# Products of constants on TensorE before each wait for gathered rows in the two relational layers

## What is computed

```python
def _rel_layer(x, src, dst, etypes, V, a, w_loop, bias, activation=None):
    W = jnp.einsum('rb,bio->rio', a, V)
    seg = dst.astype(jnp.int32) * R + etypes.astype(jnp.int32)
    agg = jax.ops.segment_sum(x[src], seg, num_segments=N * R)
    agg = agg.reshape(N, R, -1)
    h = jnp.einsum('nri,rio->no', agg, W) + x @ w_loop + bias
    if activation is not None:
        h = activation(h)
    return h
...
h = jnp.maximum(_layernorm(x, axis=-1), 0.0)
x = x + _L0_gnn_ref(h, src, dst, edge_type_20, ...)   # two _rel_layer, relu between
x = x + _L1_gnn_ref(h, edge_index, 3125)              # sum of neighbours
x = x + _L2_gnn_ref(h, edge_index, edge_attr_16, ...) # edge networks ("flow")
x = x + _L3_gnn_ref(h, ..., edge_index)               # attention
```

## Time and profile before

| | us |
|---|---|
| runs, median of 3 | 4871.88 |
| runs, lowest and highest | 4849.11, 4895.27 |
| span of the profiled execution | 4857.7 |
| busy in it: PE, PEld, DVE, ACT, POOL | 2328.2, 1793.5, 1913.1, 475.2, 2571.2 |

### The profile page before, as it was taken

One profiled execution on the slowest core, in us unless ns is written; L12 is line 12 of the kernel. 1 busy time (PEld: TensorE's weight loads), 2 busy tenths in 40 slices (PEclk: granted clock), 3 DMA queues, 4 the chain that ended last, 5 costly groups with the idle time before them and its releaser, 6 DMA issues. The chain is left out here.

```text
span 4857.7 us, 64843 instructions
## 1 busy us (share of the span) xinstructions
PE 2328.2 (48%) x20169; PEld 1793.5 (37%) x20302; DVE 1913.1 (39%) x6164; ACT 475.2 (10%) x1072; POOL 2571.2 (53%) x2544
## 2 busy tenths in 40 slices
PE   1300002332363232335556489888888455565562
PEld 0100002333343332334555355555555344344441
DVE  8000001111121111144545466665665455555557
ACT  0000000000000000000000022222222111111110
POOL 4777775666626666644554444444443444444440
PEclk9555555555555555555656699999998556656655
DMA  3211111000020000010000100000000000000010
GB/s 89 62 7 7 7 7 48 12 11 12 11 72 12 11 11 12 12 19 14 15 15 14 12 9 8 8 8 7 8 7 5 19 15 15 16 14 16 15 15 4
DMA packets 122759, 82.94 MB, mean 17 GB/s; under 512 B 75092, under 2 KB 109016, under 8 KB 122456
## 3 DMA queue, kind: packets, MB, share of 16 engines
q0 software_dynamic: 80160, 46.17, 8.2%
q1 hardware_dynamic: 42552, 36.17, 2.6%
HBM read 54.41 MB, written 27.29 MB: 17 GB/s over the span
## 5 line engine op out<-in xcount | busy, mean ns | idle before, releaser
L598 POOL DMA_INDIRECT rel_rows<-message_table,rel_index x880 | 842.5, 957 | 519.0 <-issue 277.0
L630 PE MATMUL rel_acc<-rel_rows,rel_onehot 128*128 128x32 f32 x1760 | 393.6, 372 | 872.4 <-issue 582.9
L630 PEld LDWEIGHTS rel_acc<-rel_rows,rel_onehot 128*128 128x128 f32 x1760 | 402.5, 324 | 863.5 <-issue 863.2
L1002 POOL DMA_INDIRECT flow_x<-node_table,flow_index x440 | 424.6, 965 | 548.5 <-DVE flow_index L1017 440.4
L1357 POOL DMA_INDIRECT att_kv_rows<-kv_table,att_index x440 | 421.0, 957 | 508.9 <-DVE att_index L1368 380.3
L362 POOL DMA_INDIRECT sorted_edges<-scatter_rows,scatter_index x425 | 505.4, 1189 | 131.7 <-issue 128.8
L1139 PE MATMUL flow_acc_bwd<-flow_onehot_j,flow_by_q 128*128 128x309 bf16 (+1 forms) x2508 | 557.5, 337 | 8.8 <-issue 0.4
L798 POOL DMA_INDIRECT sum_rows<-node_table,sum_index x320 | 326.3, 1020 | 295.1 <-DVE sum_index L821 195.6
L609 DVE COPY rel_index<-message_indices 128x8 uint32 x110 | 22.2, 202 | 1051.7 <-remote 956.1
L860 PE MATMUL p_sum_picked<-sum_h_parts,sum_source_onehot 128*128 128x96 bf16 x3000 | 250.6, 260 | 209.7 <-issue 204.1
L831 DVE TENSOR_SCALAR sum_source_onehot<-sum_sources,sum_node_numbers 128x384 bf16<-128x384 f16 x1000 | 235.7, 314 | 289.1 <-PE p_sum_picked L860 148.8
(11 more groups left out here) (248 smaller groups left out, 3861.8 us busy)
## 6 DMA issues: line engine op xcount, KB each, us to landing
message_table<-message_rows SPq DMA_DIRECT2D x50, 320.0 KB, 2.1
rel_rows<-message_table,rel_index POOLq DMA_INDIRECT x880
flow_x<-node_table,flow_index POOLq DMA_INDIRECT x440
att_kv_rows<-kv_table,att_index POOLq DMA_INDIRECT x440
sorted_edges<-scatter_rows,scatter_index POOLq DMA_INDIRECT x425
sum_rows<-node_table,sum_index POOLq DMA_INDIRECT x320
sorted_edges<-records SPq DMA_DIRECT2D x1, 4400.0 KB, 12.0
records<-sorted_edges SPq DMA_DIRECT2D x1, 4400.0 KB, 13.1
```

The lines of the kernel that those rows point to most:

```text
L598: pool.indirect_dma_start(out=rows[b][:, t, :], out_offset=None, in_=table, in_offset=bass.IndirectOffsetOnAxis(ap=ibuf[b][:, t:t + 1], ax ...
L630: last = pe.matmul(acc[:, bass.ds(col, F)], hot[b][:, t, :], rows[b][:, t, :], start=False, stop=True, skip_group_check=True)
L1002: pool.indirect_dma_start(out=X[b][:, t, 0:F], out_offset=None, in_=d["nodes"], in_offset=bass.IndirectOffsetOnAxis(ap=ibuf[b][:, t:t + 1] ...
```

## The change

A spare PSUM bank is taken and given back at once (no other tile of the pass asks for a bank). In each group, between the wait for the one-hots and the wait for the rows, TensorE multiplies the bf16 identity by a constant ramp of 128 numbers that is read four times, 12 times over, into that bank. Nothing reads the bank.

```diff
@@ -583,6 +583,8 @@
         hot = [sb(st, f"{name}_onehot{b}", [P, G, P]) for b in range(BUFS)]
         acc = ps(st, f"{name}_acc", [P, 2 * BANK])
+        with ExitStack() as apart:
+            spare = ps(apart, f"{name}_spare", [P, BANK])
         gathered = s["moved"][name]
@@ -624,6 +626,9 @@
                         pe.load(regs, s["dcol"][0:1, 0, bass.ds(g * G, G)])
                         pe.wait_ge(hot_ready, g + 1)
+                        for _ in range(12):
+                            pe.matmul(spare[:], s["identb"][:], s["iotab"][:].unsqueeze(1).to_broadcast([P, 4, P]),
+                                      start=True, stop=True)
                         pe.wait_ge(gathered[b], i * (16 * G) + 16 * G)
                         for t in range(G):
```

## The result

The changed kernel takes 4899.34 us (median of 20 runs, 4868.42 to 4945.57); the kernel before, timed beside it, 4870.64 us (20 runs, 4840.24 to 4905.00). The ratio is 1.0057, 95% interval 1.0034 to 1.0079. The change makes the kernel 29 us slower, 0.6%. I had forecast 4940 us, and given "slower by over 1%" the largest chance. The sign and the place were right, and the range held the time; the cost was 69 us in the forecast and is 29 us.

The account below looks back on a forecast made before the run. The prediction took GpSimd's gathers, 10.0 us per group, to bound the relational layers. Span 4857.7 + 60 for dearer stalls + 8 for layer ends = 4926 us; with the median 14 us above span, 4940 us, range 4700 to 5065 us.

Parts of the forecast that it names:

- GpSimd's gathers set the layers; quiet groups cost nothing: Relational layers: gathers take 10.0 us per group; TensorE's 8.8 or 4.5 us fits beneath when its completions are on time.
- Stretches come from unbroken gathers: Relational layers: gathers hold TensorE's completions back from about 15 us into a run; a pause of some 5 us frees them.
- the cure: Rival for the relational layers: constants keep TensorE awake, late completions and GpSimd's index waits vanish, about 4700 us; chance 0.20.
- Records count, whatever their width: During late completions in the relational layers, each TensorE load or matmul costs 1.4 us; a group has 56 instead of 32.
- The bound of 63: TensorE in the relational layers: 63 instructions issued but not completed, two groups now, 1.1 groups with the constants.
- The number of cycles: Relational layers: 110 groups give 22 cycles of late completions and pause now, 32 at the low clock with the change.
- A cycle costs 7.7 us: Relational layers: each cycle costs GpSimd 169.4/22 = 7.7 us of waiting; 32 cycles make 249 us, 80 us more.
- The clock: a mix nearer the low level: TensorE in the relational layers: between 80 us more at 1.2 GHz and no more at 2.4 GHz, so 60 us.
- Tails, 8 us: Ends of the two relational layers: TensorE's last groups, still owed after the last gather, get longer, 4 us per layer.
- Median 14 us above the span: Whole kernel: the runs' median, 4871.88 us, lies 14 us above the traced span, so 14 us is added.
- Hidden: Rival for the relational layers: the clock rises or constants don't count during late completions, all is covered, 4872 us; chance 0.25.
- TensorE-bound: Rival for the relational layers: low clock, 37 cycles with pauses of 9.5 us, 179 us more, 5065 us; chance 0.10.

Follow-up runs that it names:

- e3: Kernel before, without constants, with GpSimd filling an unused tile for 5.3 us ahead of each group's gathers in the relational layers: 5320.85 us, ratio 1.1051.
- e10: Kernel before with gathered rows split into two bf16 parts, half the TensorE instructions per group, and 11 sets of row buffers instead of 5: ratio 1.0045.
- e1: Changed kernel with the 12 constant products per group 32 columns wide instead of 512: 4829.73 against 4799.28 us for the kernel before, ratio 1.0065.
- e2: Changed kernel with 24 constant products per group instead of 12: 4861.36 us, ratio 1.0126 to the kernel before.
- e4: Kernel before with only upper bf16 halves multiplied in the relational layers, 16 TensorE instructions per group instead of 32: 4775.93 us, ratio 0.9948.
- e9: Kernel before with gathered rows split into two bf16 parts, half the TensorE instructions per group, and 5 sets of row buffers: ratio 1.0056.

## Why the prediction was right in sign and too high by 41 us

*GpSimd's gathers set the layers; quiet groups cost nothing.* Right as far as traces show: outside stretches the constants and the 16 products fit between the rows, TensorE's busy time rose by 308 us (forecast 286 to 572) and GpSimd's idle time that isn't for an index did not rise (263.2 against 277.0 us).

*Stretches come from unbroken gathers, and neither density nor clock prevents them.* Right for the layers in the batches like the one forecast from: stretch at 1090 straight behind dense work at 2.4 GHz, none in e3. Incomplete in two ways. e10 shows 556.6 us of unbroken gathers with none: I had one trace and took its behaviour for that of the hardware. And the attention layer, which I used as an argument against the cure, has late completions in 47 of 55 groups of that same trace; I had looked for slow products only.

*Records count, whatever their width, and the number outstanding is bounded.* That records count is right in the main: e1, with 6% of the columns, causes nearly as many waits; 24 and 48 records more per group and 16 fewer move "layers" by +27, +52 and -30 us. The bound of 63 was not tested.

*The number of cycles: 3.4 groups at the low clock, 5.0 at the high one.* My 32 cycles came near the 35 waits measured, but in part by luck. The formula lets TensorE run freely for 16 us and clear groups at its own pace. In e1 a group takes 3.8 us, so it gives 16/3.8 + 0.4 + 1.1 = 5.7 groups per cycle and fewer waits than before; the runs there are three groups long all the same. In the stretch shown above the changed kernel clears one group in 7.0 us (1079.30 to 1086.27) and the next in 4.5 us (to 1090.73), between the two clocks of my formula, and its cycles are three groups long too. What is alike in the commonest cycles is the number of records: 5 x 32 = 160 before, 3 x 56 = 168 in the changed kernel and in e1, 2 x 80 = 160 in e2, 10 x 16 = 160 in e4. Why a cycle takes that many isn't shown.

*A cycle costs 7.7 us.* **This is the step that failed.** I wrote "32 cycles x 7.7 = 249 us, 80 us more", with the pause of before as a constant. The 169.4 us held the first wait of 22.5 us, which is no stretch's, and beside it there were 24 waits, not 22: 146.9/24 = 6.1 us was the price even before. And the price falls when the runs get shorter: 184.0/35 = 5.3 us with the change, 4.8 to 4.9 us in its three later traces. 32 cycles at 6.1 us would have been 49 us more; at 5.3 us they are 23 us more; the 35 waits measured are 184 - 147 = 37 us more, where I had put 60 us in the sum. Of this rise not all reaches the gathers, since GpSimd's other gaps got shorter by 14 us (9 us in the mean over four traces): they took 26.0 us more. So 34 of the 41 us lie in this term. That the pause depends on the run before it is shown by the table under e2; that it is the time in which TensorE clears what it owes is my reading. The two pauses that I had printed, 5.96 and 4.30 us, were below 7.7 us already, and I didn't ask why.

*The clock: a mix nearer the low level, 60 us taken of 80.* The layers' clock came out at 0.65, within my 0.5 to 0.8, and e1 shows that it doesn't matter much: at 0.50 the ratio is the same. The interpolation between clock levels refined a quantity that wasn't the one at stake.

*Tails, 8 us.* Not borne out: means over four traces are 13.2 us before and 13.9 us with the change. That is the other 7 of the 41 us.

*Median 14 us above the span.* Each run's time lies 1.8 us above its own span, and the other 12 us were the distance of that one execution from the median. They are scatter and no cost, but adding them is right for a forecast of a median, and no part of the error lies here: the kernel before took 4870.64 us beside the changed one, against 4871.88 us in the sum.

*The rivals.* Hidden (4872 us) ended nearest in size, 27 us off against 41 for my own, though the interval excludes it. The cure is refuted by e3 and by the change itself. TensorE-bound is not reached even with 24 constants; its 5065 us are also 6 us more than its own terms add up to (4871.9 + 179 + 8 = 5059). The page that I named, "TensorE: Matmul & The Clock Gate" of the Trainium skill, section "What's actually happening", is right that activity releases the clock (0.50 to 0.65 here). What it doesn't decide is whether anyone waits for the clock.

*Chances.* "Slower by over 1%" had 0.48, and the time is within 1%, which had 0.32.

## What to carry to other kernels

Filler work for the clock is free only if nothing else that it uses is short; here it is the number of TensorE's instructions that costs, much more than their time, and 24 more of them in a group of 32 cost 0.6%. When a stall repeats in cycles, find out which part of it follows the time between two stalls and which part is paid for each, and multiply only the second by the number of cycles. Before building on a stall that the code doesn't explain, run the unchanged kernel again, at other times and on other chips: the stall here was worth 17%, and the change 0.6%.

## What the runs showed of the hardware

- In all batches but one, completions of TensorE reach the other engines late while GpSimd gathers: up to 40 us in an unbroken run in the relational layers, 5.6 us in the median in the attention layer. In the relational layers TensorE's loads and matmuls then leave some 1.4 us apart. A pause of the gathers, mostly of 3 to 9 us, frees them, and the longer the run, the longer the pause. Gathers of 64 or 128 rows give 25 waits each, products of 32 or 512 columns 34 and 36; the number of TensorE's instructions changes it.
- In the batch of e9 and e10 nothing was late with the same program, in any stage of which the steps were compared (relational and attention layers): 4018 against 4799 to 4893 us for the kernel before, with single instructions of equal length (1187 and 1187, 232 and 231, 684 and 686 ns). Whether chip, neighbours or something else made the difference isn't shown.
- What physically holds the completions back isn't settled. Every execution here was recorded while it ran. The Trainium skill, page "NOTIFIC — the notification-queue block", section "Overflow: three behaviours, one of which stalls the engine", says that the block that writes the records of instruction tracing can be set to stall the engine that produces them, when the ring of records is full, until software drains it. That would fit a cost per instruction and a difference between batches, but no run here shows how it was set, none could leave the recording out, and it is a conjecture.
- A kernel against itself gave a ratio of 0.9960 with an interval of 0.9932 to 0.9988. The interval holds the scatter from run to run, not all of it; a single stage read from the trace was the sharper measure.
